# A four-layer graph network on one core: the first dense half beside five edge stages, a residual row made at the first edges, and three rearranged stages

## The reference, cut to what matters

```python
# layer 0: three mean aggregations over incoming edges
h = relu(sage(h, b1)); h = relu(sage(h, b2)); h = sage(h, b3)     # sage = h@Wself + b + mean(h[src])@Wneigh
x1 = x + h
# layer 1: both directions, batch norm over all nodes
h = relu(layernorm(x1))
g = (mean_by_dst(h[src]-ea)@W_O + mean_by_src(h[dst]-ea)@W_I + h@W_S + biases) / 3
x2 = x1 + batchnorm(g)
# layer 2: GRU on typed messages, all nodes;  layer 3: mean of h[dst]@W over edges, by src
x3 = x2 + gru(sum_by_dst(h[src]@W_msg + type_row), h)
out = x3 + mean_by_src((h@W + b)[dst])
```

## Time and profile before

| what | value |
|---|---|
| median of 3 runs | 6115.24 us (6112.87 to 6128.49) |
| profiled execution | 6119.6 us, span of the core 6117.1 us |
| PE busy | 4614.1 us (75%), mean granted clock 0.85 |
| DVE busy | 4068.7 us (67%) |
| POOL busy | 3763.8 us (62%) |
| ACT busy | 2955.0 us (48%) |
| instructions | 111102 |

### The profile page before, as it was taken

The page is one execution under the profiler, slowest core; times in us unless marked ns, Lnnn a source line. Parts: engine busy times, 40 slices in busy tenths (PEclk is TensorE's granted clock), DMA queues, the critical chain, the costliest instruction groups (busy, mean ns, idle before and its releaser), DMA issues. The chain is left out here.

```text
span 6117.1 us, 111102 instructions
## 1 busy us (share of the span) xinstructions
PE 4614.1 (75%) x24801; PEld 3442.3 (56%) x24801; DVE 4068.7 (67%) x15478; ACT 2955.0 (48%) x6844; POOL 3763.8 (62%) x3959
## 2 busy tenths in 40 slices
PE   3895956669999998436656756999999978865564
PEld 1573644446776777435644534876666644444564
DVE  4885855556766778543257757769999989964431
ACT  0594745543773784432211101558888865544100
POOL 0466667740750660475657723768888878857687
PEclk9997967779999999657878887569999989975787
DMA  3463546659879878656756687544544445524555
GB/s 101 135 208 112 183 154 207 207 179 314 272 244 311 269 265 301 203 153 206 254 139 122 117 199 200 157 146 171 172 171 171 171 144 154 152 92 147 130 102 74
DMA packets 723459, 1102.02 MB, mean 180 GB/s; under 512 B 104051, under 2 KB 405861, under 8 KB 722940
## 3 DMA queue, kind: packets, MB, share of 16 engines
q1 hardware_dynamic: 549690, 860.18, 43.2%
q0 software_dynamic: 137600, 175.02, 13.6%
q10 hardware_dynamic: 36000, 64.94, 2.8%
HBM read 665.45 MB, written 456.37 MB: 183 GB/s over the span
## 5 line engine op out<-in xcount | busy, mean ns | idle before, releaser
L1098 POOL DMA_INDIRECT G_x<-node_table,G_idx x400 | 399.4, 998 | 567.3 <-ACT G_idx L1084 446.1
L1098 POOL DMA_INDIRECT G_V<-layer_rows,G_idx x400 | 384.7, 962 | 125.2 <-issue 114.7
L1940 POOL DMA_INDIRECT node_table<-H_out,H_idx x200 | 322.6, 1613 | 142.2 <-issue 78.4
L1127 PE MATMUL bank<-first_last_indicators,G_V 125*128 (+1 forms) x1600 | 271.5, 292 | 182.9 <-DVE G_V L1775 182.9
L1127 PEld LDWEIGHTS bank<-first_last_indicators,G_V 125*128 125x128 f32 x1600 | 275.7, 259 | 187.0 <-issue 132.7
L1940 POOL DMA_INDIRECT out<-O_out,O_idx x200 | 312.1, 1561 | 89.5 <-issue 60.5
L1475 PE MATMUL bank<-B_S,B_V 127*128 127x125 f32 x2000 | 296.9, 295 | 55.1 <-DVE B_S L1451 37.3
L2182 PE MATMUL bank<-O_r,O_eq 125*125 125x128 f32 x1592 | 229.4, 314 | 140.8 <-ACT O_out L2194 106.4
L2759 ACT ACTIVATE P_h<-P_x,P_nb,P_rs 128x128 f32<-128x128 f32 x784 | 320.3, 479 | 0.0
L1475 PEld LDWEIGHTS bank<-B_S,B_V 127*128 127x128 f32 x2000 | 265.6, 206 | 77.5 <-issue 65.1
L2182 PEld LDWEIGHTS bank<-O_r,O_eq 125*125 125x125 f32 x1592 | 222.0, 227 | 148.2 <-issue 148.1
(11 more groups left out here) (490 smaller groups left out, 15222.1 us busy)
## 6 DMA issues: line engine op xcount, KB each, us to landing
P_x<-node_table SPq DMA_DIRECT2D x196, 512.0 KB
B_V<-values SPq DMA_DIRECT2D x250, 256.0 KB, 4.0
BN_g<-node_table SPq DMA_DIRECT2D x195, 256.0 KB
out<-P_out SPq DMA_DIRECT2D x195, 256.0 KB
node_table<-G_xg SPq DMA_DIRECT2D x97, 512.0 KB
values<-G_V SPq DMA_DIRECT2D x150, 256.0 KB
layer_rows<-A_a SPq DMA_DIRECT2D x100, 256.0 KB, 3.2
layer_rows<-B_rows SPq DMA_DIRECT2D x100, 256.0 KB
```

The lines of the kernel that those rows point to most:

```text
L1098: pool.indirect_dma_start(out=rows[u][:, c, :], out_offset=None, in_=table, in_offset=bass.IndirectOffsetOnAxis(ap=idx[u][:, c:c + 1], axi ...
L1127: last = nc.tensor.matmul(m.bank[7][:, bass.ds((i * TILE + c) * 2, 2)], V[0:EP, c, :], m.ind[0:EP, bass.ds(i * TILE + c, 1), :].rearrange( ...
L1940: pool.indirect_dma_start(out=table, out_offset=bass.IndirectOffsetOnAxis(ap=idx[u][:, c:c + 1], axis=0), in_=out[u][:, c, :], in_offset=N ...
```

## The change

1. `SHARES = (43, 43, 43, 43, 24)` replaces four equal chunks: the first four dense stages have 43 groups each, and 24 groups run in `incoming`, whose engines' loops become parts of `beside`. `together` now goes on with the part that is left when the shorter one has ended.
2. `edges_start` makes x1 of each edge's source: PE adds five matmuls per tile, DVE one addition, SP one store of 256 KB to the upper half of a new table `TB3`, whose lower half is `X1`. The slots of `x_src` go from 4 to 8, and the loops of DVE, ACT and POOL are unrolled 8 times instead of 4. `incoming` gathers from `TB3` through `i_tb`; `i_src2` and the three DVE operations that make it are gone.
3. `outgoing_self`: the keys come from a matmul (`key_row`, one f16 product of 500 columns per tile, into banks 6 and 7) instead of a broadcast load, and SP issues the load of `X1` of tile i-1 behind the other loads of tile i.
4. H and O2: the key row is loaded as one window of 750 columns (250 of the tile before, 500 own), so that each of the two front columns of `eq` takes one DVE operation of 500 columns instead of two of 250. In H the scattered index is made on ACT from `i_srcf`, and the wait for the landing of tile i-4 leaves DVE.
5. `gru`: `dT` moves from POOL to DVE; the copies of the gather index move from ACT to POOL, each behind the wait for gather i-1 of its slot.

```diff
-CHUNKS = 4
+SHARES = (43, 43, 43, 43, 24)
...
 def together(eng, parts, unroll=4, back=3, ahead=3):
+    begin = min(p[0] for p in parts)
+    while parts:
+        start = unroll * -(-max(begin, back + 1) // unroll)
+        rounds = max(0, min((n - special - ahead - start) // unroll for _, n, _, special, _ in parts))
+        short = min(last for _, _, last, _, _ in parts)
+        end = start + unroll * rounds
+        stop = max(end, short + 1)
...
+        begin, parts = stop, [p for p in parts if p[2] >= stop]
...
 # edges_start, PE
+                        f.after(s_x1, i - 6)
+                        nc.tensor.matmul(r3[0:EP, :], m.ones16[:, 0:EP], m.b3parts[:], start=True, stop=False, skip_group_check=True)
+                        for c in range(TILE):
+                            last = nc.tensor.matmul(r3[0:EP, c * D:(c + 1) * D], a2T[(u - 5) % 4][:, c * EP:(c + 1) * EP], m.w["self3"],
+                                                    start=False, stop=True, skip_group_check=True)
+                        last.then_inc(s_m3, 1)
 # edges_start, DVE
+                        nc.vector.tensor_tensor(x1[v][:], r3[0:EP, :].rearrange("p (c f) -> p c f", c=TILE), xs[(w - 5) % 8][:], ALU.add)\
+                          .then_inc(s_x1, 1)
 # incoming
-                    gather(pool, f, idx, s_i, i, u, m.XE, x_whole, s_g)
+                    gather(pool, f, idx, s_i, i, u, m.TB3, x_whole, s_g)
...
+        beside(nc, m, a, P, 4, sync=sync, vector=vector, scalar=scalar, gpsimd=gpsimd, tensor=tensor,
+               sync_once=lambda sp: sp.wait_ge(m.s_ea, m.ea_copied), sync_end=lambda sp: finish(sp, s_vo, n))
 # outgoing_self, SP
-                    sum_loads(sp, m, f, i, u, V, krow, s_V, s_k, s_sel, s_agg)
-                    f.after(s_T, i - 4)
-                    sp.dma_start(r_whole[u][:], edge_rows(m.H1, i)).then_inc(s_h[u], 16)
-                    Flow(sp, has, m).landed(s_sc, i - 4, u, 64)
-                    sp.dma_start(xg_whole[u][:, :, 0:D], edge_rows(m.X1, i)).then_inc(s_x[u], 16)
+                    if has(i):
+                        value_load(sp, m, f, i, u, V, s_V, s_agg)
+                        f.after(s_T, i - 4)
+                        sp.dma_start(r_whole[u][:], edge_rows(m.H1, i)).then_inc(s_h[u], 16)
+                    if has(i - 1):
+                        v = (u - 1) % 4
+                        Flow(sp, has, m).landed(s_sc, i - 5, v, 64)
+                        sp.dma_start(xg_whole[v][:, :, 0:D], edge_rows(m.X1, i - 1)).then_inc(s_x[v], 16)
 # equal_sources
         if c >= HALF:
-            last = nc.vector.tensor_scalar(eq[u][:, c, :], krow[u][0:EP], key, weight, ALU.is_equal, ALU.mult)
+            last = nc.vector.tensor_scalar(eq[u][:, c, :], krow[u][0:EP, BLOCK:], key, weight, ALU.is_equal, ALU.mult)
+        elif f.has(i - 1):
+            nc.vector.tensor_scalar(eq[u][:, c, :], krow[u][0:EP, 0:EG], key, weight, ALU.is_equal, ALU.mult)
         else:
-            if f.has(i - 1):
-                nc.vector.tensor_scalar(eq[u][:, c, 0:BLOCK], krow[u - 1][0:EP, BLOCK:EG], key, weight, ALU.is_equal, ALU.mult)
-            nc.vector.tensor_scalar(eq[u][:, c, BLOCK:EG], krow[u][0:EP, 0:BLOCK], key, weight, ALU.is_equal, ALU.mult)
+            nc.vector.tensor_scalar(eq[u][:, c, BLOCK:], krow[u][0:EP, BLOCK:EG], key, weight, ALU.is_equal, ALU.mult)
 # gru, POOL
-                        nc.gpsimd.tensor_tensor(dT[v % 2][:], hT[v][:], nT[v][:], ALU.subtract).then_inc(s["d"], 1)
                     g = Flow(pool, has, m)
+                    next_index(nc, g, m.i_dst, idx, s_i, i + 3, u + 3, s_x)
 # gru, DVE
+                    if has(i - 6):
+                        v = (u - 6) % 4
+                        f.after(s["n"], i - 6)
+                        nc.vector.tensor_tensor(dT[v % 2][:], hT[v][:], nT[v][:], ALU.subtract).then_inc(s["d"], 1)
```

276 lines of the change are left out of this document (136 added, 140 removed).

## The result

The changed kernel takes 6187.3 us (median of 4 runs, 6181.3 to 6190.7) against 6117.8 us for the kernel before (4 runs): 1.011 times as long, 95% interval 1.0093 to 1.0128. I had forecast 6047 us. The profiled execution has a span of 6188.3 us, 71 us more than before.

The account below looks back on a forecast made before the run. POOL was taken to bound positions, lookup, `edges_start` and `incoming`, PE the first take stage, DVE `gru`. Terms -5 -14 -14 +35 +2 -25 -22 -25 = -68 us took 6115 to 6047 us; range 5985 to 6105, the forecast's own 6015 to 6085.

Parts of the forecast that it names:

- part 2: `incoming`: with 24 dense groups a common step takes 7.1 us, stage 302 us against 267, +35 us (+10 to +65).
- The slower rival: `incoming`: both pipelines add up through ACT and DVE to a 10.5 us step; kernel 6141 us, chance 0.08.
- Part 1: 43 groups instead of 49 in four stages: positions 0, lookup -5, G1 and G2 -14 us each.
- Part 3: `edges_start`: the added x1 work fits in POOL's 10.0 us a tile; +2 us (0 to +20).
- Part 4: `outgoing_self`: earlier values and H1 and no key load remove three quarters of POOL's pauses; -25 us (0 to -33).
- Part 5: H: merged `eq` shortens the round that sets the step, -22 us (-5 to -34); O2, bound by POOL's scatters, 0.
- Part 6: `gru`: `hnew` no longer held by POOL's `dT`, DVE's step 8.0 us, POOL late next; -25 us (0 to -35).

Follow-up runs that it names:

- experiment 1: The changed kernel with SyncE's dense half taken ahead of its edge half in `incoming` alone: 6043.3 us, ratio 0.988 to the kernel before.

## Why the prediction was wrong, point by point

**The step that failed** is in part 2: "SP's loads and stores share the queue in this order, the dense ones first; a tile's attributes are asked for three tiles ahead, so I cost them at 0". The edge part came first, and the load that I costed at 0 set the step: 13.86 us instead of 7.1, +186 us instead of +35. With the order that I had written down the stage measured 305.8 us against my 302, the step 7.09 us against 7.1, and the kernel 6043 us against 6047. The slower rival named the right stage and the right side (it decides from 9.7 us a step on) but the wrong chain: ACT's root and VectorE's statistics are tied in experiment 1 as well, and its step is 7.09 us.
That the total of experiment 1 comes within 4 us of the forecast is in part luck. `outgoing_self` gave 12 us more than forecast, BN 11, `gru` and the two take stages together 5 each; `incoming` cost 4 us more, H gave 5 less, and the stages without a term are 9 us longer. By the spans the difference is 80 us and by the medians 74, against my 68.

**Part 1** was right in place and near in size: lookup -3.5 (mine -5), G1 -17 and G2 -15 (-14 each), positions as long as before. The kernel before starts the next stage's first operation 23.7 us behind POOL's last gather of G1:

```profile
1821.49 0.84 DVE L1145 COPY G_shared_first_last<-bank 128x400 f32<-128x400 f32 x1 [9.34 <-PEq L257]
```

In the changed kernel the two are 9.8 us apart (timeline):

```profile
1795.58 0.95 POOL L1100 DMA_INDIRECT G_V<-layer_rows,G_idx  x1 [0.30 <-issue]
...
1805.42 0.84 DVE L1147 COPY G_shared_first_last<-bank 128x400 f32<-128x400 f32 x1 [26.70 <-PEq L264]
```

**Part 3**, `edges_start`: +4.5 us against +2.

**Part 4**, `outgoing_self`: the term was mis-sized, -37 against -25. All of POOL's pauses beyond 0.30 us went (scatters 253.9 us, 200 x 1.27 is 254), and the stage's ends shrank by 3. The prediction named both causes, the order of the loads and the load that is gone, and added them up in one term; either of them alone gives all but 3 or 4 us.

**Part 5**, H: -16 against -22, by chance near. The merged eq, on which the term rested, gave nothing that shows when it alone was undone: I had put VectorE on the round that sets the step because it waited for the counts; the 29 us that it got back moved the scatters by 0.1 us, so in the kernel with the other edits it was not on it where it counts. (36 of 50 tiles of these 29 us are 21 us and not the 22 that I wrote.) Which chain is, the runs don't single out. O2 was forecast at 0 and is 7 us longer (a scatter 1584 instead of 1561 ns); the cause is open.

**Part 6**, `gru`: -30 against -25. `hnew` fell to 0.66 us, the step to 7.85. Groups by line in `gru`, changed kernel, as in the earlier trace rows but over the whole stage:

```profile
L1100 POOL DMA_INDIRECT B_x<-node_table,B_idx x200 | 212.3, 1061 | 55.1 <-issue 52.8 <-POOL B_idx L1081 1.7 <-DVE B_ve L2562 0.6
L2505 POOL TENSOR_TENSOR B_rs<-B_ve,minus_half 125x4 f32<-125x4 f32 x50 | 68.8, 1377 | 34.6 <-DVE B_ve L2562 33.8
...
L2527 DVE TENSOR_TENSOR B_d<-B_hT,B_n 128x500 f32<-128x500 f32 x50 | 33.4, 669 | 0.0
L2554 DVE TENSOR_TENSOR B_hnew<-B_n,B_q 128x500 f32<-128x500 f32 x50 | 33.2, 663 | 0.2
```

POOL is not late next, as I had it: it waits 33.8 us for VectorE's `ve`, and VectorE still sets the step. The mechanism (one operation held by dT) is shown, but alone worth 10 us.

**Not forecast:** BN is 11 us shorter without an edit. Over the stage the DMA engines moved 286 instead of 268 GB/s. That the new table shifts the node table in memory is a guess that no run tests. It would not be the whole: in the five kernels with the keys of `outgoing_self` loaded again, which change no table, BN takes 180 to 181 us, in all other versions of the changed kernel 174 to 176, on both kinds of chip. The cause stays open.

## What to carry to other kernels

Slots give slack only if the queue that fills them does: for each load, count in steps of the engine that waits from the last wait **ahead of it in its queue**, whoever's wait that is, to its first use. A load asked for as early as its slot allows can be the worst neighbour in a shared queue.
When two reliefs feed one stall, undoing each alone shows next to nothing; undo both before calling either idle. And read an ablation by stage: the run with eq in two was slower by about the amount expected, in another stage.

## What the hardware showed that I had not expected

The place of a loop's code changes its time: `gru` took 431, 441, 444 or 448 us with the same instructions in it, with 11 to 13 packets of q14 in the short cases and 27 or 28 in the long ones, and 64 small operations ahead of the loop brought 441 back to 430. In `edges_start` 33 packets instead of 17 cost nothing: POOL's last gather ends 502.7 or 502.8 us into the stage with either.
Chips differ. Two of them (13 and 8) ran the kernel before in 6820 and 6824 us, two others in 6121 and 6122, with BN as long on both kinds and `gru` at 428 to 431 us; which stages are longer is said above. A gather's own time was the same (0.95 us). Waits of POOL in `edges_start`, experiment 1's kernel on chip 8:

```profile
POOL A_x_src L1100 <- DVE A_x L1345: 152.1, 30, 12.4
```

and on chip 2:

```profile
POOL A_x_src L1100 <- DVE A_x L1345: 2.1, 7, 0.3
```

POOL waits there for x1, which the change brought into this stage, and the DMA engines moved 167 GB/s in it instead of 219. What is slower on the second kind I can't tell from these runs. Experiment 1's kernel gains more there: its ratio is 0.9722 (0.9681 to 0.9763). The changed kernel itself was not run on it.
